# Feed-forward bias: from a matmul in PSUM to a GpSimd add in SBUF

## What is computed

```python
z = x_flat @ ternary_quant(W_syn).T + b_syn
topv, _ = jax.lax.top_k(z, k)
thresh = topv[:, -1:]
hidden = jnp.where(z >= thresh, jax.nn.relu(z), 0.0)
out = hidden @ ternary_quant(W_out).T + b_out
return layernorm(x + out, gamma, beta)

x = x + 0.5 * _L0_ffn_ref(_layernorm(x), ...)
x = x + _L0_attn_ref(_layernorm(x), ...)
x = x + 0.5 * _L0_ffn_ref(_layernorm(x), ...)
```

## Time and profile before

| | |
|---|---|
| median of 3 runs | 1232.84 us (1231.51 to 1233.9) |
| the profiled execution | 1232.99 us |
| its span on the core | 1231.2 us |
| mean granted TensorE clock | 0.969 |
| first pass, attention, second pass | about 0 to 360, 360 to 890, 890 to 1231 us |

### The profile page before, as it was taken

How to read it: one execution, slowest core, us unless ns; L and a number is a source line. 1 busy time by engine, 2 the same in 40 slices (tenths; PEclk the granted TensorE clock), 3 DMA queues, 4 the chain that set the end, 5 groups by cost and what they waited for, 6 DMA issues and landing times.

```text
span 1231.2 us, 18036 instructions
## 1 busy us (share of the span) xinstructions
PE 1085.9 (88%) x5940; PEld 491.1 (40%) x5990; DVE 899.1 (73%) x2229; ACT 804.3 (65%) x1193; POOL 362.5 (29%) x388
## 2 busy tenths in 40 slices
PE   0788999988899799999999799999799899998886
PEld 0343455544443233232343223322244345554443
DVE  4788888889985887884326988782234888889893
ACT  5489889888645355567415356567247988988862
POOL 2101244344551441001310450002100124434456
PEclk9999999999999899999999799999899999999998
DMA  9200000002000221110001211100000000000000
GB/s 368 94 1 1 2 1 1 2 1 57 1 1 8 71 61 32 48 36 1 1 21 31 71 45 45 33 31 2 1 1 1 1 1 18 19 18 19 18 18 35
DMA packets 22287, 37.45 MB, mean 30 GB/s; under 512 B 5398, under 2 KB 7833, under 8 KB 21532
## 3 DMA queue, kind: packets, MB, share of 16 engines
q1 hardware_dynamic: 21404, 34.54, 8.9%
q0 software_dynamic: 768, 1.57, 0.5%
HBM read 19.17 MB, written 4.21 MB: 19 GB/s over the span
## 4 chain that ended last, share of the span: by engine, by line
PE 60%; DVE 21%; issue 7%; POOL 3%; ACT 3%; SPq 3%; DMA 1%; DVEq 1%; another core or an unknown queue 0%; POOLq 0%; ACTq 0%
PE zP L509 13%; PE oP L561 9%; PE xP L679 5%; PE oP L679 5%; PE zP L607 5%; PE zP L663 5%; PE hP L644 3%; DVE arena L1271 3%; DVE m L1279 3%; PE hP L531 2%; PE zP L704 2%; PE hP L704 2%; DVE scored L1476 2%; PE zP L644 2%; PE zP L613 1%
## 5 line engine op out<-in xcount | busy, mean ns | idle before, releaser
L817 ACT ACTIVATE arena<-arena,X 128x2048 int8<-128x2048 f32 x154 | 307.9, 2005 | 4.7 <-DVE X L1251 4.7
L874 ACT ACTIVATE arena<-zP,asc 128x512 f32<-128x512 f32 (+3 forms) x384 | 200.9, 583 | 110.1 <-PE zP L667 78.5
L509 PE MATMUL zP<-T,arena 128*128 128x512 f16 x1024 | 248.8, 387 | 0.7
L561 PE MATMUL oP<-T,arena 128*128 128x512 f16 x832 | 199.7, 384 | 1.4 <-DVE arena L1366 1.4
L509 PEld LDWEIGHTS zP<-T,arena 128*128 128x128 f16 x1024 | 102.2, 100 | 122.9 <-issue 11.5
L773 ACT ACTIVATE arena<-zP,sc 128x512 f32<-128x512 f32 x128 | 87.5, 688 | 86.8 <-PE zP L514 54.2
L663 PE MATMUL zP<-arena 98*128 98x512 f16 (+3 forms) x384 | 111.7, 338 | 2.9 <-DMA arena<-arena 1.9
L561 PEld LDWEIGHTS oP<-T,arena 128*128 128x128 f16 x832 | 82.0, 99 | 79.6 <-issue 5.5
L1498 DVE RECIPROCAL arena<-arena 128x128 f32<-128x128 f32 x64 | 57.1, 926 | 61.8 <-ACT arena L887 61.8
L644 PE MATMUL hP<-arena 96*128 96x512 f16 (+3 forms) x256 | 84.5, 353 | 15.6 <-DVE mx L1476 12.2
L990 POOL TENSOR_SCALAR ln<-ln 128x1 f32<-128x1 f32 x32 | 38.6, 1205 | 198.0 <-DVE ln L1195 197.8
(11 more groups left out here) (203 smaller groups left out, 1840.6 us busy)
## 6 DMA issues: line engine op xcount, KB each, us to landing
arena<-arena SPq DMA_DIRECT2D x168, 64.0 KB, 2.0
arena<-in_w_synT SPq DMA_DIRECT2D x4, 1024.0 KB, 8.1
arena<-in_w_outT SPq DMA_DIRECT2D x4, 1024.0 KB, 14.8
out_dram<-x_sb SPq DMA_DIRECT2D x16, 256.0 KB, 2.0
x_sb<-in_x SPq DMA_DIRECT2D x3, 1024.0 KB, 14.0
arena<-in_w_o SPq DMA_DIRECT2D x2, 1024.0 KB, 5.0
arena<-arena POOLq DMA_DIRECT2D x24, 64.0 KB, 1.9
arena<-in_b_syn SPq DMA_DIRECT2D x1, 1024.0 KB, 11.9
```

The costliest lines, as they stand in the source:

```text
L509: pe.matmul(zP[:, c * CW:(c + 1) * CW], part[:, g % 2, k, :], T1[:, k, c * CW:(c + 1) * CW], start=(n == 0 and k == 0), stop=False)
L561: mm = pe.matmul(o, part[:, k, :], T2[:, k, :], start=(c == 0 and n == 0 and k == 0), stop=False)
L817: act.activation(junk[:, counted[0] % 2, :], Z[:, g % ZR, :], ACT.Sign, bias=X[:, 2, k:k + 1], accum_out=S[:, k:k + 1]).then_inc(sm["cnt"], 1)
L874: act.activation(PT[:, m // 4 % 2, h, q0:512], colP[m % 3][:, q0:512], ACT.Exp, scale=asc[:, g, 10:11]).then_inc(sm["exp_done"], 1)
```

## The change

- The bias matmul L514 of every chunk goes (128 in all), and with it b_syn's part of `bias_parts`, of `bcol`, `bpart` and `brow`, and one of SP's trips through DRAM.
- At the start GpSimd forms `bz` = `bsyn` times SH, 128x2048 float32, with one tensor_scalar in slot 0. SP writes one row of it to DRAM.
- A GpSimd stage `add_bias` adds a chunk of `bz` to the same chunk of `Z`, in place, 128x512, four per tile. Each waits for its chunk's `evac`. Its places in GpSimd's slot are seen in the diff.
- The first count of a tile (`count` with k = 0) waits for the four adds (`z_set`) instead of the four evacuations, on ScalarE; the counts on VectorE too.
- `bz` lies in the last 2048 words of `arena`, which the attention part uses. SP therefore loads it again from DRAM, broadcast to all partitions (1 MB), in the second batch of the attention, after the last row maxima and ahead of the barrier; the second pass's first add waits for it.

The diff, cut to its core:

```diff
@@ sync @@
-            for n, (lo, j, first) in enumerate(((0, 16, 0), (16, 4, N))):
-                eng.wait_ge(sm["bpart_set"], 3 * n + 3)
...
+            eng.wait_ge(sm["bz_set"], 1)
+            eng.dma_start(bz_row.rearrange("(o n) -> o n", o=1), bz[0:1, :]).then_inc(sm["bz_out"], 16)
...
+                if b == 1:
+
+                    eng.wait_ge(sm["bz_out"], 16)
+                    eng.wait_ge(sm["attn_set"], TOTAL["norm"] + 4)
+                    eng.wait_ge(sm["bo_added"], 2 * BT)
+                    eng.wait_ge(sm["mrow_in"], 16 * HG * 2 * TOTAL["turn"])
+                    eng.dma_start(bz, bz_row.partition_broadcast(P)).then_inc(sm["bz_in"], 16)
@@ tensor, mm1 @@
-                        pe.matmul(zP[:, c * CW:(c + 1) * CW], part[:, g % 2, k, :], T1[:, k, c * CW:(c + 1) * CW],
-                                  start=(n == 0 and k == 0), stop=False)
-                if g == 0 and c == 0:
-                    pe.wait_ge(sm["bones_set"], 3)
-                    pe.wait_ge(sm["brow_in"], 16)
-                pe.matmul(zP[:, c * CW:(c + 1) * CW], bones[:, :], brow[:, c * CW:(c + 1) * CW],
-                          start=False, stop=True).then_inc(sm["z_ps"], 1)
+                        mm = pe.matmul(zP[:, c * CW:(c + 1) * CW], part[:, g % 2, k, :], T1[:, k, c * CW:(c + 1) * CW],
+                                       start=(n == 0 and k == 0), stop=(n == 1 and k == KD - 1))
+                mm.then_inc(sm["z_ps"], 1)
@@ scalar, count; the same in count_here on vector @@
-                    act.wait_ge(sm["z_evac"], 4 * g + 4)
+                    act.wait_ge(sm["z_set"], 4 * g + 4)
@@ gpsimd @@
+            def add_bias(f, i, c):
+                g = f * NT + i
+                if (i, c) == (0, 0):
+                    pool.wait_ge(sm["bz_in"] if f else sm["bz_set"], 16 if f else 1)
+                pool.wait_ge(sm["z_evac"], 4 * g + c + 1)
+                z = Z[:, g % ZR, c * CW:(c + 1) * CW]
+                pool.tensor_tensor(z, z, bz[:, c * CW:(c + 1) * CW], ALU.add).then_inc(sm["z_set"], 1)
...
                     do(final, f, s, S_FIN + 1)
+                    do(add_bias, f, s, 2, 3)
+                    do(add_bias, f, s, 1, 0)
                     do(rstd2, f, s, S_FIN)
                     do(rstd1, f, s, -1)
+                    do(add_bias, f, s, 1, 1)
+                    do(add_bias, f, s, 1, 2)
                     if f == 0 and s == 0:
+                        pool.wait_ge(sm["scales_set"], 1)
+                        pool.tensor_scalar(bz, bsyn[:, :], SH, None, ALU.mult).then_inc(sm["bz_set"], 1)
@@ vector, start @@
-            link(dve.reciprocal(RC1, SC1))
-            dve.wait_ge(sm["bcol_in"], 32)
-            bias_parts(0, 16, RC1, 0)
```

More of the change, by code:

```diff
@@ L176, in program @@
         flags, flagsT = carve(32), carve(32)
+        assert taken[0] <= ARENA - N
+        bz = arena[:, ARENA - N:ARENA]
         taken[0] = 0
@@ L200, in program @@
         tail = taken[0]
+        assert tail == ARENA - N
         w_lat = carve(5 * 256).rearrange("p (k n) -> p k n", k=5)
@@ L212, in program @@
         bo = carve(D)
-        brow = sb("brow", [P, N + D], BF16)
+        brow = sb("brow", [P, D], BF16)
         bones = sb("bones", [P, P], BF16)
-        bcol = sb("bcol", [P, 20], F32)
-        bpart = sb("bpart", [P, 3, 20], BF16)
-        btmp = sb("btmp", [P, 32], F32)
+        bcol = sb("bcol", [P, 4], F32)
+        bpart = sb("bpart", [P, 3, 4], BF16)
+        btmp = sb("btmp", [P, 8], F32)
         flagi = sb("flagi", [P, 1], I32)
@@ L257, in program @@
         SC1, THR, NTHR, S1, S2, SH, SC2, SIG, T0 = (sc[:, i:i + 1] for i in range(9))
-        RC1, RC2, ZSC = sc[:, 25:26], sc[:, 26:27], sc[:, 27:28]
-        b_rows = nc.dram_tensor("b_rows", (3, N + D), BF16, kind="Internal").ap()
+        RC2, ZSC = sc[:, 26:27], sc[:, 27:28]
+        b_rows = nc.dram_tensor("b_rows", (3, D), BF16, kind="Internal").ap()
+        bz_row = nc.dram_tensor("bz_row", (N,), F32, kind="Internal").ap()
         names = ("vec_in x_first x_in0 x_in1 x_in2 x_in3 w1_in0 w1_in1 w1_in2 w1_in3 w2_in0 w2_in1 w2_in2 w2_in3 "
                  "ones_set ident_set consts_set abs_done sum_ps sum_read tern_done sq_done scales_set search_set "
-                 "brow_in orow_in bcol_in bpart_set brow_out bones_set "
+                 "bz_set bz_out bz_in z_set orow_in bcol_in bpart_set brow_out bones_set "
                  "stats1 xn_done rstd1 xT_ps xT_hi xT_lo z_ps z_evac upd cnt below_set ok_set ok_sum ok_read "
@@ L410, in _ @@
                     eng.dma_start(x_sb[:, 0, :], xv[:, 0, :]).then_inc(sm["x_first"], 16)
-            eng.dma_start(bcol[:, 0:16], b_syn.rearrange("(p j) -> p j", j=16)).then_inc(sm["bcol_in"], 16)
-            eng.dma_start(bcol[:, 16:20], b_out.rearrange("(p j) -> p j", j=4)).then_inc(sm["bcol_in"], 16)
+            eng.dma_start(bcol[:, :], b_out.rearrange("(p j) -> p j", j=4)).then_inc(sm["bcol_in"], 16)
             for v, d in ((b_syn, bsyn), (gamma, gam), (beta, bet)):
@@ L422, in _ @@
                 eng.dma_start(x_sb[:, 4 * c:4 * c + 4, :], xv[:, 4 * c:4 * c + 4, :]).then_inc(sm[f"x_in{c}"], 16)
-            for n, (lo, j, first) in enumerate(((0, 16, 0), (16, 4, N))):
-                eng.wait_ge(sm["bpart_set"], 3 * n + 3)
[L425 to L430, removed]
+            eng.wait_ge(sm["bz_set"], 1)
+            eng.dma_start(bz_row.rearrange("(o n) -> o n", o=1), bz[0:1, :]).then_inc(sm["bz_out"], 16)
+            eng.wait_ge(sm["bpart_set"], 3)
+            for r in range(3):
+                eng.dma_start(b_rows[r, :].rearrange("(p j) -> p j", j=4), bpart[:, r, :]).then_inc(sm["brow_out"], 16)
+            eng.wait_ge(sm["brow_out"], 48)
+            eng.wait_ge(sm["bones_set"], 2)
+            eng.dma_start(brow[0:3, :], b_rows).then_inc(sm["orow_in"], 16)
             eng.wait_ge(sm["hT_ps"], 4 * 11)
@@ L563, in mm2 @@
                 if c == 3:
+                    pe.wait_ge(sm["bones_set"], 3)
                     pe.wait_ge(sm["orow_in"], 16)
-                    mm = pe.matmul(o, bones[:, :], brow[:, N:N + D], start=False, stop=True)
+                    mm = pe.matmul(o, bones[:, :], brow[:, :], start=False, stop=True)
                 mm.then_inc(sm["mm2"], 1)
@@ L1120, in scale_of, with bias_parts @@
                 link(dve.tensor_scalar(NTHR, THR, -1.0, None, ALU.mult))
-            def bias_parts(lo, hi, inverse, done):
-                v = [bpart[:, r, lo:hi] for r in range(3)]
-                u, w = btmp[:, 0:hi - lo], btmp[:, 16:16 + hi - lo]
-                link(dve.tensor_scalar(u, bcol[:, lo:hi], inverse, None, ALU.mult))
+            def bias_parts(inverse):
+                v = [bpart[:, r, :] for r in range(3)]
+                u, w = btmp[:, 0:4], btmp[:, 4:8]
+                dve.wait_ge(sm["bcol_in"], 16)
+                link(dve.tensor_scalar(u, bcol[:, :], inverse, None, ALU.mult))
                 dve.tensor_copy(v[0], u).then_inc(sm["bpart_set"], 1)
-                dve.wait_ge(sm["bpart_set"], done + 1)
+                dve.wait_ge(sm["bpart_set"], 1)
                 link(dve.tensor_tensor(w, u, v[0], ALU.subtract))
                 dve.tensor_copy(v[1], w).then_inc(sm["bpart_set"], 1)
-                dve.wait_ge(sm["bpart_set"], done + 2)
+                dve.wait_ge(sm["bpart_set"], 2)
                 dve.tensor_tensor(v[2], w, v[1], ALU.subtract).then_inc(sm["bpart_set"], 1)
```

7 lines of the change are left out of this document (3 added, 4 removed).

## The result

1300.95 us, median of 4 runs (1299.55 to 1301.94), against 1233.36 (1231.51 to 1233.9, 4 runs) for the kernel before: a ratio of 1.055, interval 1.0532 to 1.0568. It is slower by 5.5%, inside the range and 7 us above the forecast of 1294. The profiled execution took 1301.85 us with a span of 1299.9, 68.7 more than the span before.

What follows compares the result with a forecast made beforehand. TensorE ends last in full slots, with VectorE 0.84 us behind, so VectorE's blocking by GpSimd's adds decides. Terms 19 + 9 + 22 + 2 - 3 + 12 = +61 on 1232.99 give 1294 us; range 1258 to 1318 (80%).

Steps and rivals of the forecast that it cites:

- TensorE and VectorE are level at 16.4 us once the matmuls are gone: Full slots of 17.25 us: without 0.86 of bias matmuls TensorE needs 16.4; VectorE, less 0.84 idle, also 16.4.
- An add of GpSimd and an operation of VectorE with two SBUF inputs, or a scalar or copy one on several elements, exclude each other: Wherever GpSimd's adds meet such VectorE operations: blocked for a whole instruction, costing 0.9 to 1.0 us each.
- the second rival: Adds collide only at L1204, L1383 and L1284, while `update` slips between them: +31, 1264 us; chance 15%.
- Full slots, 2.7 less 0.84: Slots 10 to 14, both passes: 2.7 us of VectorE lost, less 0.84 idle, 1.9 per slot; +19 (10 to 28).
- Slots 15 to 17: Both passes: losses of 2.7, 2.7 and 0.9, less 1.7 of idle time, twice; +9 (6 to 13).
- Slots 3 to 9 of the first pass and 6 to 9 of the second: Slots without `final`, 3.9 us lost each, VectorE nearly without pause in the first pass: +22 (12 to 27), +12 (7 to 16).
- the discount: In those slots without `final`: half an add off per slot, since the fourth waits for ScalarE and may miss `update`.
- First pass, start: +2: Start and slots 1 and 2: -2.9 from the first bias matmul, against 4 to 6 adds at 0.9; +2 (-3 to +6).
- the relief: First pass, start: the first chunk's bias matmul, which waited 2.24 us and took 0.59, goes; -2.9.
- The row bz, counted 0: First pass, start: GpSimd's tensor_scalar forming bz takes 6.3 us but does not block VectorE; 0.
- Second pass, slots 1 to 5: -3: TensorE sets these 11.64 us slots; adds are hidden, 5 x 0.86 us come back, fifth half covered; -3 (-4 to +3).
- The bz reload: Second pass: bz fetched again, 1 MB on SP's queue, lands before the first add near 893 us; 0.

Runs made afterwards that it cites:

- e1: The changed kernel with every GpSimd add cut to 16 columns, waits and order kept, bias left out elsewhere; 1443.94 us, with VectorE's exact search running.
- e9: Against the changed kernel: GpSimd adds only chunks 0 and 3, from the fifth tile, behind the flag; other bias matmuls return, ScalarE makes bz; 1223.34 us, ratio 0.9927.
- e7: The changed kernel with the row bz formed by a ScalarE activation instead of GpSimd's tensor_scalar; 1293.88 us, ratio 1.049.
- e5: The changed kernel with each GpSimd add replaced by a one-input tensor_scalar (z times 1), bias left out; 1452.26 us, with VectorE's exact search running.

## Why the prediction was right, and where a term was off

- *TensorE and VectorE are level at 16.4 us once the matmuls are gone.* Right: e1 measured 16.39 and 16.5.
- *An add of GpSimd and an operation of VectorE with two SBUF inputs, or a scalar or copy one on several elements, exclude each other; the blocked one gets in between two adds.* Right, for operands down to 4 elements (L1258), which the second rival had doubted. Prices: 0.87 at L1225 (0.9 foretold), 0.94 at L1404 and L1305 (0.9), 1.07 in `update` (1.0).
- *Full slots, 2.7 less 0.84.* Right: +1.96 per slot in the second pass, and +1.6 in the first, so 17.9 in place of 19. The adds cost somewhat less in the first pass (2.5 against 2.7).
- *Slots 15 to 17.* Right, 8.3 for 9.
- *Slots 3 to 9 of the first pass and 6 to 9 of the second.* "Nearly without a pause" was a misreading: before the change VectorE was busy for 72.1 of these 86.5 us. But 7.1 of the 14.4 idle ones are its wait for GpSimd's `rstd1`, and 2.3 the gaps between small operations, and both stood on the same chain, so that the blocking came on top of them: VectorE became busy for 28.5 us more and idle for only 2.8 less. So the mechanism was right, the discount was not: I took off half an add per slot, since the fourth "may then miss `update`". The four ran without a pause and hit four instructions (the early slot above). Without the discount of 3.5 the first pass' term is 25.5 (measured 25.7), and without 2 the second's is 14 (14.5). The slots differ among themselves, by 2.4 to 4.9 us in the first pass; the last of them lost most, since it ends with a pair on L1225 and L1404 as a full one does.
- *First pass, start: +2.* This is the step that failed: +7.3 measured. Of its parts, the relief gave about 1.9 for 2.9 foretold (e1 starts slot 3 at 64.39, of which bz holds 5.06: 59.33 against 61.19). The adds cost 68.53 - 64.39 = 4.1 (4 to 6 at 0.9 foretold). The row bz, counted 0, cost 5.06. The reading behind the 0 was one instruction, L1171 beside L1078. The instruction just ahead of it, L1170, took 0.49 us beside the same GpSimd operation (last section), and I passed that over. One short row could not carry "does not block", and the high end of +6 for the whole start was too low with it.
- *Second pass, slots 1 to 5: -3.* About right. The stretch that holds them got shorter by 4.6, but 1.5 of it lie ahead of the second pass, in a part that varied by 2.8 us from one trace to another (598.0 in e9, 600.8 in e7); from the first `normal` of the second pass on it is -3.1. The fifth slot lost half of its 0.86 us, as foretold (11.18, where 11.64 was before). The sum in the text was loose: 5 x 0.86 less half of one is 3.9, not 3.
- *The bz reload.* Nothing of it shows: slot 1 of the second pass starts no later, and the stretch that holds it got shorter.

The errors are +5.3 at the start, +3.7 and +2.5 in the early slots, -1.1, -0.7, -1.6 and -0.4 elsewhere: +7.7, the distance from +61 to +68.7. That the total came within 7 us is in part luck, 11.5 us too low in some terms against 3.8 too high in others; the terms of the full slots were right by themselves.

## What to carry to other kernels

Before work is given to GpSimd, don't ask how idle it is; ask which of VectorE's instructions will start while it runs. Beside a GpSimd tensor_tensor each such instruction that reads two SBUF tensors or is a scalar or copy operation within SBUF loses the rest of the GpSimd instruction, down to 4 elements here, so an add of 1.25 us costs VectorE about a microsecond per instruction hit. And where GpSimd runs freely behind a semaphore that VectorE waits on too, the collision comes in every iteration: a wait put ahead of it, or the choice of which chunks it gets, can be worth more than the work moved (33 us for one wait here, against about 28 us of matmuls taken from TensorE).

## What was not expected of the hardware

- A blocked instruction of VectorE gets in between two GpSimd adds that are 1.25 us apart, in every slot shown, and once two more small ones with it. A pair of adds therefore costs two instructions, not one of double length, and a chain of small dependent operations is hit again and again.
- A tensor_scalar of GpSimd blocked a VectorE tensor_scalar for all of its 5.48 us in one place (5.64 us for 0.55) and for 0.33 us of 1.5 in others. In e5, with 128 of the short ones, it depends on when VectorE's instruction starts. One early in it (timeline of e5):

```profile
67.86 1.49 POOL L1028 TENSOR_SCALAR arena<-arena 128x512 f32<-128x512 f32 x1
...
67.95 0.54 DVE L1256 TENSOR_SCALAR arena<-X 128x8 f32<-128x8 f32 x1
68.41 0.16 DVE L1257 TENSOR_SCALAR arena<-X 128x8 f32<-128x8 f32 x1
```

  In the whole trace, small operations that started 0.03 to 0.23 us behind a GpSimd one of this length ended 0.62 to 0.64 us behind its start. Those that started after 0.54 to 0.96 us took their usual time. Scalar and copy operations that started after 1.0 us or more waited for GpSimd's end again, while small tensor_tensors of two SBUF inputs that started in the same part took their usual 0.13 to 0.17. So a short one blocks at its start and at its end and leaves its middle open. The one of 5.48 us shows no open middle, and why stays open. In the trace of before, VectorE's small operations beside L1078 took 0.16 us, all but one:

```profile
48.27 1.57 POOL L1078 TENSOR_SCALAR gam<-gam 128x512 f32<-128x512 f32 x1
...
48.42 0.49 DVE L1170 TENSOR_TENSOR sc<-sc 128x1 f32<-128x1 f32 x1
...
49.22 0.16 DVE L1176 TENSOR_SCALAR X<-sc 128x5 f32<-128x5 f32 x1
```

  In the changed kernel the same operations beside the same one of GpSimd took longer:

```profile
51.27 1.50 POOL L1098 TENSOR_SCALAR gam<-gam 128x512 f32<-128x512 f32 x1
...
52.20 0.59 DVE L1197 TENSOR_SCALAR X<-sc 128x5 f32<-128x5 f32 x1
52.27 0.52 DVE L1199 SCALAR_TENSOR_TENSOR Bk<-sc 128x5 f32<-128x5 f32 x1
```

  These end near 52.79, when L1098 does, and they start 0.93 and 1.00 us behind its start; L1176 started 0.95 us after L1078 and was free. L1170 ended 0.64 us after L1078's start, as in e5. No run was made that tells what differs between the two ends.
